# Second batch's gathers through eight places, its finishing one tile sooner

## The reference

```python
h = _layernorm(x) * (1 + ca) + sa
x = x + ga * attention(h, Wqkv, temp, Wout, bout)     # linear-time attention over token statistics
h = _layernorm(x) * (1 + cb) + sb
x = x + gb * ffn(h, ...)
```

```python
shared = _swiglu(xf, sW1, sW2, sW3)
h = silu(einsum('td,efd->etf', xf, eW1)) * einsum('td,efd->etf', xf, eW3)
eo = einsum('etf,edf->etd', h, eW2)
specialist = einsum('te,etd->td', combine, eo)        # combine has topw at the two chosen experts
return X + (shared + specialist)
```

## Time and profile before

| | us |
|---|---|
| median of 3 runs | 1375.05 |
| lowest and highest | 1368.68, 1376.51 |
| profiled execution, its own time | 1379.95 |
| its span, first to last instruction | 1377.1 |
| PE busy | 1257.0 |
| DVE busy | 1063.2 |
| ACT busy | 877.3 |
| POOL busy | 363.0 |
| last gather starts (L1718) | 1368.8 |

### The profile page before, as it was taken

One profiled execution on the slowest core, in us unless ns is written; L12 is line 12 of the kernel. 1 busy time (PEld: TensorE's weight loads), 2 busy tenths in 40 slices (PEclk: granted clock), 3 DMA queues, 4 the chain that ended last, 5 costly groups with the idle time before them and its releaser, 6 DMA issues.

```text
span 1377.1 us, 18860 instructions
## 1 busy us (share of the span) xinstructions
PE 1257.0 (91%) x5880; PEld 899.6 (65%) x5880; DVE 1063.2 (77%) x2304; ACT 877.3 (64%) x1399; POOL 363.0 (26%) x424
## 2 busy tenths in 40 slices
PE   3985768999999999999999999999998999999994
PEld 2443545666667666676765676766666888788873
DVE  4856757988988887888986987898965876568755
ACT  2655756777878767776788776677678654343431
POOL 0088531001000011101001100001750206866544
PEclk9998878999999999999999999999999999999997
DMA  5001027000000000000000001201321526656454
GB/s 207 8 1 62 1 107 260 5 9 5 5 8 5 5 9 5 5 5 8 5 9 12 17 12 29 74 5 28 111 85 62 177 90 205 209 177 184 146 151 144
DMA packets 73211, 91.24 MB, mean 66 GB/s; under 512 B 18493, under 2 KB 60542, under 8 KB 72860
## 3 DMA queue, kind: packets, MB, share of 16 engines
q1 hardware_dynamic: 59066, 61.49, 14.1%
q0 software_dynamic: 8832, 25.18, 6.1%
q10 hardware_dynamic: 5218, 3.39, 0.8%
HBM read 48.15 MB, written 41.80 MB: 65 GB/s over the span
## 4 chain that ended last, share of the span: by engine, by line
PE 74%; DVE 12%; ACT 7%; issue 3%; ACTq 1%; POOL 1%; another core or an unknown queue 1%; DMA 0%; POOLq 0%; DVEq 0%
PE PS L2000 10%; PE PS L1923 8%; PE PS L1926 8%; PE PS L1940 7%; PE PS L1943 7%; PE PS L1941 7%; PE PS L1875 7%; PE PS L2030 5%; DVE mx L1254 4%; DVE PL L1300 3%; PE PS L1861 2%; PE PS L1792 2%; PE PS L1984 2%; PE PS L2013 2%; PE PS L1888 2%
## 5 line engine op out<-in xcount | busy, mean ns | idle before, releaser
L1254 DVE TENSOR_REDUCE mx<-PS 128x1 f32<-128x512 f32 x512 | 343.6, 683 | 53.0 <-PE PS L1875 50.4
L874 ACT ACTIVATE PT<-PS 128x1024 f32<-128x1024 f32 x256 | 262.4, 1025 | 181.3 <-PE PS L1926 178.7
L1300 DVE TENSOR_TENSOR PL<-PT,PH 128x512 fp32r<-128x512 f32 x512 | 358.6, 707 | 17.9 <-ACT PH L877 17.1
L877 ACT ACTIVATE PH<-PT 128x1024 fp32r<-128x1024 f32 x256 | 271.5, 1061 | 8.1
L1940 PE MATMUL PS<-PH,VH 128*65 128x512 f32 x512 | 213.7, 417 | 1.8 <-ACT OZ L888 1.7
L1943 PE MATMUL PS<-PL,VH 128*65 128x512 f32 x512 | 202.7, 396 | 0.0
L1941 PE MATMUL PS<-PH,VL 128*65 128x512 f32 x512 | 202.3, 395 | 0.0
L1641 POOL TENSOR_TENSOR O<-OZ,Z 64x512 f32<-64x512 f32 x30 | 42.0, 1399 | 527.5 <-DMA Z<-z_scratch 520.1
L1875 PE MATMUL PS<-KA,Q 128*128 128x512 f32 x384 | 153.5, 410 | 11.8 <-DVE mx L1254 8.7
L1923 PE MATMUL PS<-Q,KA 128*128 128x512 f32 x384 | 130.2, 420 | 3.2 <-DMA Q<-mT 3.2
L1926 PE MATMUL PS<-Q,KB 65*128 65x512 f32 x384 | 122.0, 399 | 0.0
(11 more groups left out here) (263 smaller groups left out, 2442.7 us busy)
## 6 DMA issues: line engine op xcount, KB each, us to landing
xbuf<-xT SPq DMA_DIRECT2D x26, 384.0 KB, 4.4
nxT<-in_wexp SPq DMA_DIRECT2D x9, 768.0 KB, 4.6
xg<-xbuf SPq DMA_DIRECT2D x52, 128.0 KB
ybuf<-nxT SPq DMA_DIRECT2D x44, 128.0 KB
ybuf<-yo SPq DMA_DIRECT2D x34, 128.0 KB
x<-in_x SPq DMA_DIRECT2D x8, 512.0 KB, 12.2
x_scratch<-x SPq DMA_DIRECT2D x2, 2048.0 KB, 7.3
nxT<-norm_scratch POOLq DMA_DIRECT2D x32, 128.0 KB
```

The source lines that it names most:

```text
L874: act.activation(PT[:, gs % 4, :], PS[:, bk:bk + 2, :].rearrange("p a n -> p (a n)"), ACT.Exp, scale=0.125).then_inc(sem("pt"), 1)
L877: act.activation(PH[:, gs % 4, :], PT[:, gs % 4, :], ACT.Copy).then_inc(sem("pt_h"), 1)
L1254: dve.tensor_reduce(mx[:, qb % 2, i, c:c + 1], PS[:, k, :], AX, ALU.max).then_inc(sem("dve_out"), 1)
L1300: dve.tensor_tensor(PL[:, gs % 4, cols], PT[:, gs % 4, cols], phf[:, gs % 4, cols], ALU.subtract).then_inc(sem("pl"), 1)
```

## The change

Gathers of batch 1 go through eight places instead of four. The first four are those of `y12`; the other four are slots 4 to 11 of `rest`, two slots each, where the rows of x lay. `pair_at(n)` gives the place, `paired(n)` the semaphore and count of a landing (places 4 to 7 use the four semaphores `d_sl`, which the loads of scattered rows used earlier). A gather waits for the last finish that used its place; one that goes to places 4 to 7 also waits for all totals (`t_x2` at 16). Batch 0 keeps its four places. The finishing of batch 1 starts at step 98, not 99, so step 111 holds finish 29, and 30 and 31 come behind it.

```diff
-            (NT + 2 * NTI + 5, 1, finish_jobs(1))]
+            (NT + 2 * NTI + 4, 1, finish_jobs(1))]
...
+    pairs = [y12[:, s, :, :] for s in range(NG)] + [rest[:, 4 + 2 * q:6 + 2 * q, :] for q in range(4)]
...
+    def pair_at(n):
+        return n % NG if n < NT else (n - NT) % len(pairs)
+
+    def paired(n):
+
+        s = pair_at(n)
+        had = 32 * sum(pair_at(m) == s for m in range(n + 1))
+        return (sem(f"d_pair{s}"), had) if s < NG else (sem(f"d_sl{s - NG}"), 16 * NB * NT // NSX + had)
...
         def finish(n):
-            b, i, s = n // NT, n % NT, n % NG
-            w.wait_ge(sem(f"d_pair{s}"), 32 * (n // NG + 1))
+            b, i, y = n // NT, n % NT, pairs[pair_at(n)]
+            w.wait_ge(*paired(n))
...
         def gather(n):
-            b, i, s = n // NT, n % NT, n % NG
+            b, i, s = n // NT, n % NT, pair_at(n)
...
-            if n >= NG:
-                w.wait_ge(sem("comb"), n - NG + 1)
+            if s >= NG:
+                w.wait_ge(sem("t_x2"), 16)
+            had = [m for m in range(n) if pair_at(m) == s]
+            if had:
+                w.wait_ge(sem("comb"), had[-1] + 1)
             for j in range(2):
                 pool.indirect_dma_start(
-                    out=y12[:, s, j, :], out_offset=None, in_=ybuf[b],
-                    in_offset=bass.IndirectOffsetOnAxis(ap=slot[:, b, j, i:i + 1], axis=0)).then_inc(sem(f"d_pair{s}"), 16)
+                    out=pairs[s][:, j, :], out_offset=None, in_=ybuf[b],
+                    in_offset=bass.IndirectOffsetOnAxis(ap=slot[:, b, j, i:i + 1], axis=0)).then_inc(paired(n)[0], 16)
```

More of the change, by code:

```diff
@@ L1514, in finish @@
         def finish(n):
-            b, i, s = n // NT, n % NT, n % NG
-            w.wait_ge(sem(f"d_pair{s}"), 32 * (n // NG + 1))
+            b, i, y = n // NT, n % NT, pairs[pair_at(n)]
+            w.wait_ge(*paired(n))
             w.wait_ge(sem("gate"), b + 1)
             w.wait_ge(sem("t_x2"), 2 * (n // 4 + 1))
-            mark(dve.scalar_tensor_tensor(X2[:, n, :], y12[:, s, 0, :], gate[:, b, 0, i:i + 1], X2[:, n, :], ALU.mult, ALU.add))
+            mark(dve.scalar_tensor_tensor(X2[:, n, :], y[:, 0, :], gate[:, b, 0, i:i + 1], X2[:, n, :], ALU.mult, ALU.add))
             w.wait_ge(own, made[0])
-            dve.scalar_tensor_tensor(X2[:, n, :], y12[:, s, 1, :], gate[:, b, 1, i:i + 1], X2[:, n, :], ALU.mult,
+            dve.scalar_tensor_tensor(X2[:, n, :], y[:, 1, :], gate[:, b, 1, i:i + 1], X2[:, n, :], ALU.mult,
                                      ALU.add).then_inc(sem("comb"), 1)
```

## The result

| | before | after |
|---|---|---|
| median of 11 runs each, same chip | 1375.34 | 1380.25 |
| lowest and highest | 1368.68, 1378.62 | 1375.59, 1383.23 |
| ratio, 95% interval | | 1.0034 [1.0019, 1.0048] |
| profiled execution, its own time | 1379.95 | 1378.28 |
| its span | 1377.1 | 1376.4 |

The changed kernel is slower by 4.9 us, 0.34%. The forecast was 1370.6 and a range up to 1377: wrong, and on the wrong side. The two profiled executions alone would mislead, since the changed one reached its first gather 3.7 us earlier, before anything that the change touches. So times are counted from that gather. Behind the last matmul 6.2 us were won; ahead of it 9.1 were lost; 3.0 us net.

The account below looks back on a forecast made before the run. The prediction took the end to be bound by late gathers, each waiting for finish n - 4 to free one of four places. Terms -4.8 + 0.1 + 0.3 = -4.4 us from the median 1375.05 gave 1370.6; range 1366 to 1377.

Parts of the forecast that it names:

- Eight places, pace: Batch 1's gathers on GpSimd: issues 1.25 us apart, sixteen gathers in 40 us, over 14.2 us earlier.
- Eight places, gates: Gathers 24 to 31 wait for finishes 16 to 23, never binding; tightest is gather 31, margin 1.3 us.
- The end: Behind the last matmul: no finish waits for a landing, last finish done 4.8 us sooner.
- The 4.0 us from the last finish to the end of the span: End of the span: 4.0 us holding the last store, kept, with 0.1 us added for closer stores.
- The finish moved ahead, 0.3: Step 98: the finish moved there delays a catching-up stretch, cost taken as 0.3 us.
- The gathers' bytes are the same, and only their time moves: Queues in general: waits and instructions per engine hardly change, gathers only shift in time; no cost in the sum.
- rival B: Last stage: transfers cause more TensorE halts, 5.1 us each, giving 1375.7, or 1380.8 with two; chance 0.07.
- The prediction's own sign of being wrong, a last matmul moved by more than 1 us: TensorE's last matmul over 1 us from 1364.6, relative to the stage's start, would mean halts, not places.
- Rival D: Steps 98 to 107: finishes contend with gathers, 10.4 us, giving 1381.0, or 1375.8 half hidden; chance 0.03.

Follow-up runs that it names:

- e2: Kernel before, four places, with only the finishing moved from step 99 to 98: 1372.86 us, ratio 0.9995.
- e5: Changed kernel with batch 1's gathers fetching 64 bytes a row instead of 1024, on chip 2: 1358.23 us, ratio 0.9996 to the kernel before.
- e8: Changed kernel with GpSimd clearing 768 columns before each gather issue of batch 1, on chip 2: 1378.96 us, ratio 1.0149 to the kernel before.
- e9: Kernel before, unedited, run again on chip 1: 1373.84 us, ratio 0.9996.
- e15: Changed kernel with five places instead of eight, finishing from step 98: 1371.63 us, ratio 0.9987 to the kernel before.
- e10: Changed kernel, unedited, run again on chip 1: 1378.11 us, ratio 1.0021 to the kernel before.
- e1: Changed kernel, eight places, with the finishing back at step 99: 1378.47 us, ratio 1.0028 to the kernel before.
- e3: Changed kernel with six places instead of eight, finishing from step 98: 1374.32 us, ratio 0.9999 to the kernel before.
- e17: Changed kernel, eight places, with a one-row plain transfer behind each pair of gathers of batch 1: 1373.71 us, ratio 1.0001 to the kernel before.
- e18: Changed kernel with six places and a one-row plain transfer behind each pair of gathers of batch 1: 1373.24 us, ratio 0.9997 to the kernel before.
- e11: Changed kernel with batch 1's gathers fetching 64 bytes a row, on chip 1: 1377.27 us, ratio 1.0037 to the kernel before.

## Why the prediction was wrong

By its own steps.

- Eight places, pace. Right: 1.25 us an issue, back to back for eighteen issues.
- Eight places, gates. Wrong: "the gates do not bind" rested on the old times of the finishes, with 1.3 us of margin. The finishes depend on TensorE, and TensorE was held up; gather 25 waited 6.02 us. The last issue started 49.4 us behind the first, forecast 38.8, before 53.3. It cost nothing in itself, since the last matmul had moved further still.
- The end. Right in kind: no landing is waited for, and the last finish is over 4.2 us behind the last matmul, forecast 3.6, before 8.5.
- The 4.0 us from the last finish to the end of the span. Mis-sized: 2.2. I took them for the last store. They were GpSimd's: in the kernel before its last gather issue ends at 1369.72 and its closing event comes at 1376.94, 7.22 us later, while SyncE is through with its stores at 1375.02. That interval is the same, 7.22 to 7.24 us, in e2, e5, e8, e9 and e15. With the last gather out early it lies inside the work, and 1.9 us more are won than forecast.
- The finish moved ahead, 0.3. Harmless: e2 gives 0.9995 [0.9978, 1.0012]; 0.3 us is below what this can tell.
- "The gathers' bytes are the same, and only their time moves", priced at nothing. This is the step that failed. It is rival B's mechanism (halts grow), which had a chance of 0.07 and decides from 4.4 us of growth: the stage grew by 9.1 us, from 49.1 to 58.2, in the first pair of traces and by 13.0 in the second (e9, e10). The prediction's own sign of being wrong, a last matmul moved by more than 1 us, named the halts for this case. But B was argued by the wrong cause, the transfers' load. Its counter-evidence, TensorE busy 80.5 of 81 us beside batch 0's sixteen gathers, tells of gathers that are spread out and not of gathers issued run on. The four places seem to have been a brake that works by itself: while TensorE's signals are held up, no finish frees a place, so the gathers pause (seven times, 16.5 us), and TensorE recovers. The pauses that I read as pure waste would be that. Shown is that the loss grows with the places (e1, e2, e3), and that it is gone when plain transfers stand between at a slightly slower pace (e17, e18); that TensorE recovers because of each pause is read from the timelines, and no run sets a single pause by itself.
- Rival D. The Trainium skill, "SBUF — State Buffer", section "Who interferes with whom", says that a DVE instruction with two SBUF inputs contends with a GpSimd instruction that reads SBUF. If a gather's reading of its indices counted as such a read, gathers would lengthen a finish. The rows of the finishes after (columns: busy, mean ns, idle) speak against that reading:

```profile
L1532 DVE SCALAR_TENSOR_TENSOR X<-y,gate,X 128x256 f32<-128x256 f32 x8 | 3.9, 486 | 0.3
...
L1530 DVE SCALAR_TENSOR_TENSOR X<-nxT,gate,X 128x256 f32<-128x256 f32 x8 | 3.8, 476 | 0.0
L1530 DVE SCALAR_TENSOR_TENSOR X<-y,gate,X 128x256 f32<-128x256 f32 x8 | 3.8, 476 | 0.0
```

Sum again: -6.2 behind the last matmul (forecast -4.8 + 0.1), +9.1 ahead of it (forecast +0.3), +3.0 from the first gather on in the profiled pair; the medians of eleven runs say +4.9, and the second pair of traces (e9, e10) +5.5. Two executions of the kernel before differ by 3.0 in the same stretch (61.6 and 58.6), which is enough for the difference between the two figures.

What stays open is how a run of indirect issues delays TensorE's completions. The waiting engines have all that they need except TensorE's signal, its instructions are on record before the signal comes, and the DMA engines are not full. No run here looks inside that. One rival wasn't tested: the recording. Of the landing events that the kernel's transfers should leave, 16 each, the four traces of chip 2, which has no hold-up, hold 92%, and the others 66 to 74%. Every execution timed here comes with a recorded span and clock, so none tells whether the recording has a part in the hold-up.

## What to carry to other kernels

Before removing waits, compare the stage with its undisturbed length: here the last stage took 49.1 us where 35.5 are needed, more loss than the whole end that the change was after, and the row to look for was a stretch with the same issues in another order. A wait that goes through the victim can be a brake; take it away only when what it brakes is known to be harmless. Indirect transfers from GpSimd are best spread, here with a plain one behind each pair (3.4 us lost for 21.0 with eight places, 2.8 for 17.9 with six), and the last should be out 8 us before the end. And a variant run on a chip that doesn't show the effect tells nothing of it: compare a stretch that no edit touches first.

## What the runs showed of the hardware

- Indirect issues following each other go with late completions of TensorE, by up to 9.5 us at a time in the changed kernel (ScalarE's longest wait; 10.9 in e10) and 11.5 in e11, whether rows have 64 or 1024 bytes and issues 64 or 128 rows. With a one-row plain transfer of 0.55 us behind each pair, at 1.57 us an issue on average, no such wait is left; a memset of 0.33 us before each issue, at 1.44, leaves 18.5 us lost. In the Trainium skill, "SBUF — State Buffer", section "Who interferes with whom", PE and ACT never wait on anyone. The traces don't contradict that, since nothing shows that these waits are for SBUF; but whoever reads it as "TensorE is safe from GpSimd" is wrong by 22 us here.
- Chips differ: the kernel before took 1359.3 us on one and 1372.9 to 1375.3 elsewhere. On the first, TensorE was busy all of 1183 to 1197 in each of four traces, elsewhere 10.3 to 11.8 us of the 14; eight places of thin gathers lost 0.1 us of the stage there and 19.3 on another. The change itself wasn't timed on that chip, and may well pay there.
- GpSimd's closing came 7.2 us after the end of its last indirect issue where that issue came late (e2, e5, e8, e9, e15 and before), and 9.1 us after it in e17 and e18, where a plain issue follows.
